# Two top-2 expert stages cut into blocks of 128 rows instead of 256

## The chip, the cores and the metric

The kernel runs on 1 core of a Trainium2 chip as one program. The metric is the device time of one execution in microseconds (us). Three executions of the kernel before took 8042.65, 8048.82 and 8052.29 us. Of its engines, TensorE is called PE (PEld is its weight load), VectorE DVE, ScalarE ACT, GpSimd POOL, and SyncE SP, the engine that issues most of the loads.

## The reference

The input is a graph of 3125 nodes with 256 features (all float32) and 50000 edges. The network has four layers; each is a graph part and a feed-forward part, both added to x. Three of the feed-forward parts matter here, because all three run through the same function of the kernel.

- Layer 1 (`_L1_ffn_ref`): a router picks the top 2 of 8 private experts for each row, and a shared expert is added. Each private expert is `gelu(x @ W1 + b1) @ W2 + b2` with W1 of 256 x 1024 and W2 of 1024 x 256.
- Layer 2 (`_L2_ffn_ref`): the top 2 of 6 experts, each of three 256 x 256 products: `h1 = relu(x @ w1 + b1)`, `h2 = relu(h1 @ w2 + b2)`, `out = h2 @ w3 + b3`.
- Layer 3 (`_L3_ffn_ref`): one hidden product that all experts share, `H = gelu(x @ W1 + b1)` with W1 of 256 x 1024, and then, for the one best of 8 experts, `H @ Wd[e] + bd[e]`.

In layers 1 and 2 there are 2 x 3125 = 6250 pairs of a row and an expert.

## The kernel before, in words

The kernel is a sequence of phases with a barrier between them. A feed-forward part is four phases: `logits`, `route`, `expert_blocks`, `combine`. The stages of layers 1, 2 and 3 have the names e3, e5 and e7 in what follows (the names that `program` gives them at lines 2440, 2451 and 2459).

`route` sorts the pairs by expert and pads each expert's rows to whole blocks. It writes the rows to a buffer in memory (xbuf), and the list of which expert owns which block to `k.block_expert` (lines 971 to 981). `block_count` (line 715) gives the number of blocks for the worst case, `(pairs + experts * (size - 1)) // size`, made even; that many blocks are always worked through. With 256 rows this is 32 for e3 and 30 for e5. Stage e7, with one pair a row, has had blocks of 128 rows (32 of them) already.

`expert_blocks` (line 1052) works through the blocks with two slots of buffers, so blocks 0, 2, 4, ... use slot 0 and blocks 1, 3, 5, ... slot 1. `NR` is the number of 128-row pieces in a block: 2 for 256 rows, 1 for 128. For each block:

- SP (lines 1089 to 1100) reads the expert's number and waits until the block that used the slot before is done, by the count `ydone`. Then it issues the load of the block's rows (L1094), the loads of the expert's weights and biases (L1097, L1098, L1099), and the last bias, spread over 128 partitions (L1100). The weights are loaded for every block, also where the expert is the same as before. Where the first product's weights are common to all experts (e7), they are loaded once (L1087).
- PE waits for all loads of the slot (L1118). It makes the hidden products (L1129), then turns the next block's rows (L1112, which needs only their load), and then makes the last product (L1139), 128 rows at a time.
- ACT applies the activation to each hidden piece of 128 columns (L1166) and copies the turned rows (L1157).
- DVE adds the last bias to each 128-row result (L1187) and raises `ydone`; POOL issues the store of the block (L1196).

The wait that governs the loads is this one:

```
sp.wait_ge(ydone, NR * B + 2 - NR)
sp.dma_start(xb[:, s, :, :], xbuf[ds(B * size, size), :]...
```

`ydone` starts at 2 and rises by `NR` with each block, so for both sizes the loads of block B are issued when block B-2 is done, that is when block B-1 can start.

Of the kernel before, what the change touches and what calls it, by code (L numbers as in the profile page):

```python
# [5 lines left out]
ALU = mybir.AluOpType  # L6
ACT = mybir.ActivationFunctionType
F32 = mybir.dt.float32
BF16 = mybir.dt.bfloat16
I32 = mybir.dt.int32  # L10
# [4 lines left out]
P = 128  # L15
N_NODES = 3125
# [15 lines left out]
CAP = 489  # L32
CAP_ROWS = 512
MAX_BLOCKS = 48
HEADS, STATES, TAPS, RANK = 4, 16, 4, 16
CH = 400
NCH = NP // CH
# [669 lines left out]
BLOCK = 2 * P  # L707
# [7 lines left out]
def block_count(pairs, experts, size=BLOCK):  # L715

    n = (pairs + experts * (size - 1)) // size
    return n + n % 2
# [183 lines left out]
def route(nc, name, k, lg, E, kind, xbuf, nblocks, beside=None, steps=0, share=None, size=BLOCK):  # L902
# [6 lines left out]
    with Phase(nc, name) as ph:  # L909
# [6 lines left out]
        nb_i, nb, endb, startb = ph.sb("nb_i", [P, EE], I32), ph.sb("nb", [P, EE]), ph.sb("endb", [P, EE]), ph.sb("startb", [P, EE])  # L916
        pos, base, kept, tgt = ph.sb("pos", [P, N]), ph.sb("base", [P, N]), ph.sb("kept", [P, N]), ph.sb("tgt", [P, N])
        tgt_u = ph.sb("tgt_u", [P, N], U32)
        trash = ph.sb("trash", [P, N])
        ow = ph.sb("ow", [1, MAX_BLOCKS])  # L920
        if share is not None:
            sh = SharedExpert(ph, k, share)
        pp = ph.ps("pp", [P, 2 * C, 512])
# [3 lines left out]
        with nc.Block() as b:  # L927
            @b.vector
            def _(v):
                c = Chain(v, dve)  # L930
# [34 lines left out]
                if kind == "capacity":  # L965
                    c(v.tensor_scalar(startb[:, :], k.expert[:, 0, 0:EE], float(CAP_ROWS), None, ALU.mult))
                    c(v.memset(ow[:, :], 0.0))
                    for e in range(EE):
                        c(v.memset(ow[:, e * (CAP_ROWS // BLOCK):(e + 1) * (CAP_ROWS // BLOCK)], float(e)))
                else:  # L970
                    c(v.tensor_scalar(nb[:, :], incl[:, N - 1, :], float(size - 1), None, ALU.add))
                    c(v.tensor_copy(nb_i[:, :], nb[:, :]))
                    c(v.tensor_scalar(nb_i[:, :], nb_i[:, :], size.bit_length() - 1, None, ALU.arith_shift_right))
                    c(v.tensor_copy(nb[:, :], nb_i[:, :]))
                    c(v.tensor_tensor_scan(endb[:, :], k.ones[:, 0:EE], nb[:, :], 0.0, ALU.mult, ALU.add))
                    c(v.tensor_tensor(startb[:, :], endb[:, :], nb[:, :], ALU.subtract))
                    c(v.memset(ow[:, :], -1.0))
                    for e in range(EE):
                        c(v.scalar_tensor_tensor(ow[:, :], k.iota[0:1, 0:MAX_BLOCKS], startb[0:1, e:e + 1], ow[:, :], ALU.is_ge, ALU.add))
                    c(v.tensor_scalar(startb[:, :], startb[:, :], float(size), None, ALU.mult))  # L980
                c(v.tensor_copy(k.block_expert[:, :], ow[:, 0:MAX_BLOCKS]))
                c(v.tensor_tensor(before[:, :, :], before[:, :, :], incl[:, :, :], ALU.add))
                c(v.tensor_tensor(before[:, :, :], before[:, :, :], tot[:, :, :], ALU.subtract))
                c(v.tensor_tensor(before[:, :, :], before[:, :, :], oh[:, :, :], ALU.mult))
# [218 lines left out]
def combine(nc, name, k, ybuf, C):  # L1203


    with Phase(nc, name) as ph:
        staged, landed, added, passed = ph.sem("staged"), ph.row_dmas(G, 16 * C * NG), ph.sem("added"), ph.sem("passed")
        ix, rows = ph.sb("ix", [P, G], U32), ph.sb("rows", [P, G, D])
        with nc.Block() as b:  # L1209
            @b.gpsimd  # L1210
            def _(g):
                with g.Fori(0, C * NG) as i:  # L1212
                    for j in range(G):
                        g.wait_ge(staged, i * G + j + 1)  # L1214
                        g.sem_inc(passed, 1)  # L1215
                        g.indirect_dma_start(rows[:, j, :], None, ybuf, bass.IndirectOffsetOnAxis(ap=ix[:, j:j + 1], axis=0)).then_inc(landed[j].sem, 16)  # L1216

            @b.vector
            def _(v):
                for j in range(G):  # L1220
                    v.tensor_copy(ix[:, j:j + 1], k.back[:, j:j + 1]).then_inc(staged, 1)  # L1221
                for q in range(C):
                    with v.Fori(0, NG) as i:
                        for j in range(G):
                            xt = k.x[:, ds(i * G + j, 1), :].rearrange("p a d -> p (a d)")
                            n = q * NT + i * G + j
                            landed[j].wait(v, 16 * i + 16 * q * NG + 16)
                            v.wait_ge(added, n)
                            v.scalar_tensor_tensor(xt, rows[:, j, :], k.coef[:, ds(i * G + j + q * NT, 1)], xt, ALU.mult, ALU.add).then_inc(added, 1)  # L1229
                            v.wait_ge(added, n + 1)  # L1230
                            v.tensor_copy(ix[:, j:j + 1], k.back[:, ds(i * G + j + q * NT + G, 1)]).then_inc(staged, 1)  # L1231
# [1145 lines left out]
def program(nc, a, out):  # L2377
    k = Keep()
    with ExitStack() as ctx:
        def sb(name, shape, dt=F32):  # L2380
            return ctx.enter_context(nc.sbuf_tensor(name, shape, dt))

        def dram(name, shape, dt=F32):
            return nc.dram_tensor(name, shape, dt).ap()
# [10 lines left out]
        by_dst = (sb("d_gi", [P, SP_], U32), sb("d_kl", [P, SP_]), None, sb("d_own", [1, SP_], I32))  # L2395
        k.lg, k.expert, k.small = sb("lg", [P, NT, 8]), sb("expert", [P, NT, 9]), sb("small", [P, NT])
        k.coef, k.back = sb("coef", [P, 3 * NT]), sb("back", [P, 3 * NT + G], U32)
        k.block_expert = sb("block_expert", [1, MAX_BLOCKS], I32)
        xbuf, ybuf = dram("xbuf", (MAX_BLOCKS * BLOCK + 3 * NP, D)), dram("ybuf", (MAX_BLOCKS * BLOCK, D))
        RowDma.values.clear()  # L2400
        nc.row_dma = [ctx.enter_context(nc.semaphore(f"row_dma{j}", n)) for j, n in enumerate(ROW_DMAS)]
# [7 lines left out]
        def edges(v):  # L2409
            return v.rearrange("(p c) -> p c", c=EC)  # L2410
# [5 lines left out]
        with ExitStack() as once:  # L2416
            sort_s = SlotScatter(nc, "by_src", once, rec_s, by_src, k.deg_out)
            sort_edges(nc, k, edges(a["src"]), edges(a["dst"]), edges(a["edge_weight"]), sort_s, sort_d, xbuf[0:MAX_BLOCKS * BLOCK, :], a["node_vec"], vrow)

# [13 lines left out]
        for l in range(3):  # L2433
# [1 line left out]
            transform(nc, f"t2{l}", k, k.t, a["L1_gnn_W"][l], "next" if l < 2 else "last", a["L1_gnn_b"][l], table)  # L2435
        normalise(nc, "n3", k, keep=True, dest=k.t)
        logits(nc, "g3", k, D, a["L1_ffn_Wr"], None, 8, k.lg[:, :, 0:8])
        nb = block_count(2 * N_NODES, 8)
        route(nc, "r3", k, k.lg[:, :, 0:8], 8, "shared", xbuf, nb, share=[a["L1_ffn_" + n][8] for n in ("W1", "b1", "W2", "b2")])
        expert_blocks(nc, "e3", k, xbuf, ybuf, nb, [(a["L1_ffn_W1"], a["L1_ffn_b1"], ACT.Gelu)], (a["L1_ffn_W2"], a["L1_ffn_b2"]))  # L2440
        combine(nc, "c3", k, ybuf[0:nb * BLOCK, :], 2)

        normalise(nc, "n4", k, scale=k.dinv, table=table, dest=k.t)
        aggregate(nc, "a4", k, by_dst, table, k.t, False)
# [1 line left out]
        batch_norm(nc, k, a["L2_gnn_gamma"], a["L2_gnn_beta"])  # L2446
        normalise(nc, "n5", k, keep=True, dest=k.t)
        logits(nc, "g5", k, P, a["L2_ffn_router_w2"], a["L2_ffn_router_b2"], 6, k.lg[:, :, 0:6], ACT.Relu, a["L2_ffn_router_w1"], a["L2_ffn_router_b1"])
        nb = block_count(2 * N_NODES, 6)
        route(nc, "r5", k, k.lg[:, :, 0:6], 6, "soft2", xbuf, nb)  # L2450
        expert_blocks(nc, "e5", k, xbuf, ybuf, nb, [(a["L2_ffn_expert_w1"], a["L2_ffn_expert_b1"], ACT.Relu), (a["L2_ffn_expert_w2"], a["L2_ffn_expert_b2"], ACT.Relu)],
                      (a["L2_ffn_expert_w3"], a["L2_ffn_expert_b3"]))
        combine(nc, "c5", k, ybuf[0:nb * BLOCK, :], 2)
        attention_layer(nc, k, a, by_dst, (xs, ys, zs, bc, heads, kl_rows, x_kept, y_kept))
        normalise(nc, "n7", k, keep=True, dest=k.t)
        logits(nc, "g7", k, 1024, a["L3_ffn_Wg"], a["L3_ffn_bg"], 8, k.lg[:, :, 0:8], ACT.Gelu, a["L3_ffn_W1"], a["L3_ffn_b1"])
        nb = block_count(N_NODES, 8, P)
# [64 lines left out]
```

## Time and profile before

| | us |
|---|---|
| median of the runs (lowest, highest) | 8048.82 (8042.65, 8052.29) |
| profiled execution | 8045.51 |
| its span in the profile | 8043.8 |
| PE busy in the span | 5186.8 (64%) |
| DVE busy | 3702.6 (46%) |
| POOL busy | 3884.8 (48%) |
| ACT busy | 1376.3 (17%) |

The phases follow each other, so these shares are averages over stages with different limits; a stage has to be read by itself. The times below are from the start of the span. A "granted clock" of 1.00 is TensorE at 2.4 GHz and 0.50 is 1.2 GHz. In the trace each float32 matmul stands as two MATMUL instructions.

### The profile page before, as it was taken

How to read it: one execution, taken by the hardware profiler on the slowest of the kernel's cores; microseconds unless marked ns; L12 is line 12 of the kernel's file. 1: busy time of each engine (PE TensorE's matmuls, PEld its weight loads, DVE VectorE, ACT ScalarE, POOL GpSimd, SP SyncE). 2: the span in 40 equal slices, each digit the busy share in tenths (PEclk: the TensorE clock that was granted, in tenths of full speed). 3: DMA queues.
4: the chain of work that ended last, by engine and by line, in shares of the span. 5: the costliest groups of instructions: out<-in, count | busy, mean ns of one | idle time of the engine just before them, and what ended most of it. 6: DMA issues, size and time to landing. Idle time of an engine off the chain costs nothing. (4 is left out here: it accounts for less than half of the span.)

```text
span 8043.8 us, 98143 instructions
## 1 busy us (share of the span) xinstructions
PE 5186.8 (64%) x20419; PEld 3885.2 (48%) x20420; DVE 3702.6 (46%) x10494; ACT 1376.3 (17%) x3853; POOL 3884.8 (48%) x3967
## 2 busy tenths in 40 slices
PE   1230688373388888889799778837465666617667
PEld 0120566262266666667588656625332444414356
DVE  8994455200355455454400155440445888853311
ACT  0000000110000000000223200012144555511233
POOL 3777777677577577577200267611432444410011
PEclk9999756686555665655899855568676777758788
DMA  2011333242233333334135433305432444420035
GB/s 91 2 10 18 89 105 84 69 124 48 74 104 105 95 105 105 95 104 102 46 121 192 151 102 104 91 26 181 143 98 62 125 126 124 112 84 11 7 121 163
DMA packets 434465, 747.31 MB, mean 93 GB/s; under 512 B 107906, under 2 KB 293772, under 8 KB 432204
## 3 DMA queue, kind: packets, MB, share of 16 engines
q0 software_dynamic: 169984, 401.24, 18.8%
q1 hardware_dynamic: 264396, 345.13, 13.3%
q8 instruction: 29, 0.48, 0.0%
q14 instruction: 56, 0.46, 0.0%
HBM read 645.17 MB, written 100.02 MB: 93 GB/s over the span
## 5 line engine op out<-in xcount | busy, mean ns | idle before, releaser
L594 PE MATMUL a_pa<-a_oh,a_rows 128*128 128x128 f32 x8320 | 2281.1, 429 | 663.2 <-DVE a_oh L558 288.8
L548 POOL DMA_INDIRECT a_rows<-table,a_ix x2080 | 1976.1, 950 | 830.7 <-issue 569.3
L594 PEld LDWEIGHTS a_pa<-a_oh,a_rows 128*128 128x128 f32 x8320 | 1797.6, 303 | 1146.8 <-issue 663.0
L581 DVE TENSOR_TENSOR t_sb<-t_sb,a_pa 128x256 f32 x2080 | 874.7, 421 | 1091.4 <-PE a_pa L594 995.7
L1808 POOL DMA_INDIRECT mx_at_rows<-heads,mx_at_ix x416 | 497.4, 1196 | 700.1 <-PE mx_at_pa L1854 587.9
L1187 DVE TENSOR_TENSOR e_ys<-e_py,e_bl 128x256 f32<-128x256 f32 x188 | 78.7, 424 | 1399.2 <-PE e_py L1139 1101.1
L1196 POOL DMA_DIRECT2D ybuf<-e_ys x110 | 74.3, 675 | 1013.7 <-DVE e_ys L1187 1008.1
L1129 PE MATMUL e_phid<-e_xt,e_w 128*128 128x256 f32 (+1 forms) x2800 | 531.7, 348 | 49.1 <-DMA e_bl<-in_L_ffn_expert_b 27.3
L196 POOL DMA_INDIRECT rec_s<-by_src_rstage,by_src_tstage x400 | 485.7, 1214 | 152.4 <-issue 107.7
L196 POOL DMA_INDIRECT rec_d<-by_dst_rstage,by_dst_tstage x400 | 474.5, 1186 | 153.6 <-issue 115.1
L1139 PE MATMUL e_py<-e_wl,e_h 128*128 128x256 f32 x2288 | 529.2, 388 | 6.9 <-DVE e_ys L1187 6.8
L644 ACT COPY t_ast<-t_sb 128x256 f32 x125 | 45.5, 403 | 2768.4 <-PEq L85 2727.6
L1129 PEld LDWEIGHTS e_phid<-e_xt,e_w 128*128 128x128 f32 x2800 | 461.5, 194 | 113.4 <-issue 63.4
L1139 PEld LDWEIGHTS e_py<-e_wl,e_h 128*128 128x128 f32 x2288 | 437.6, 196 | 67.5 <-DVE e_ys L1187 7.2
L1166 ACT ACTIVATE e_h<-e_phid,e_b 128x256 f32<-128x256 f32 (+1 forms) x760 | 329.2, 437 | 716.5 <-PE e_phid L1129 701.8
L502 PE MATMUL n_pt<-ident,n_stage 128*128 128x128 f32 x350 | 111.1, 446 | 517.2 <-DVE n_stage L478 516.7
L556 DVE TENSOR_SCALAR a_oh<-iota,d_kl 128x128 f32<-128x128 f32 x1696 | 362.0, 301 | 179.2 <-issue 179.2
L1854 PE MATMUL mx_at_pa<-mx_at_rows,mx_at_oh 128*128 128x260 f32 x832 | 297.2, 483 | 171.2 <-DVE y_sb L1790 87.1
L1875 ACT ACTIVATE mx_at_rows<-mx_at_rows 128x64 f32<-128x64 f32 x1664 | 406.3, 333 | 0.0
L397 PE MATMUL es_pdeg<-es_ohhi,es_ohlo 125*128 125x25 bf16 x800 | 145.8, 203 | 354.1 <-DVE es_ohhi L356 309.8
L502 PEld LDWEIGHTS n_pt<-ident,n_stage 128*128 128x128 f32 x350 | 51.7, 205 | 576.5 <-DVE n_stage L478 576.4
L2130 PE MATMUL mx_pmm<-mx_work,ident 128*128 128x320 f32 x640 | 301.1, 638 | 0.0
(472 smaller groups left out, 5951.4 us busy)
## 6 DMA issues: line engine op xcount, KB each, us to landing
mx_work<-bc SPq DMA_DIRECT2D x160, 320.0 KB, 3.4
e_w<-in_L_ffn_W SPq DMA_DIRECT2D x33, 1024.0 KB
a_rows<-table,a_ix POOLq DMA_INDIRECT x2080, 2.7
e_wl<-in_L_ffn_W SPq DMA_DIRECT2D x32, 1024.0 KB
e_wl<-in_L_ffn_Wd SPq DMA_DIRECT2D x32, 1024.0 KB
e_xb<-xbuf SPq DMA_DIRECT2D x78, 256.0 KB, 2.7
ybuf<-e_ys POOLq DMA_DIRECT2D x78, 256.0 KB, 4.0
e_w<-in_L_ffn_w SPq DMA_DIRECT2D x16, 1024.0 KB
```

The source lines that it names most:

```text
L196: g.indirect_dma_start(self.rec, bass.IndirectOffsetOnAxis(ap=self.tstage[:, j:j + 1], axis=0), self.rstage[:, j, :], None).then_inc(self. ...
L548: g.indirect_dma_start(rows[:, j, :], None, table, bass.IndirectOffsetOnAxis(ap=ix[:, j:j + 1], axis=0)).then_inc(landed[j].sem, 16)
L556: ins = v.tensor_scalar(oh[:, j, :], k.iota[:, 0:P], kl[:, ds(col, 1)], None, ALU.is_equal)
L581: v.tensor_tensor(acc[:, :, ts(tile, P)], acc[:, :, ts(tile, P)], pa[:, j % NB, 0:D].rearrange("p (k n) -> p k n", k=KD), ALU.add).then_in ...
L594: mm = pe.matmul(pa[:, j % NB, q * P:(q + 1) * P], rows[:, j, q * P:(q + 1) * P], oh[:, j, :], start=True, stop=True)
L1129: mm = pe.matmul(phid[:, (offs[l] + f) % NB, 0:size], ws[l][:, sl, q, f * P:(f + 1) * P], src, start=q == 0, stop=q == kt - 1)
L1139: mm = pe.matmul(py[:, (s * NR + n) % 2, 0:D], hs[-1][:, q, n * P:(n + 1) * P], wls[:, s, q, :], start=q == 0, stop=q == KL - 1)
L1166: a.activation(hs[l][:, f, :], phid[:, (offs[l] + f) % NB, 0:size], hidden[l][2], bias=bs[l][:, sl, f:f + 1]).then_inc(hact, 1)
L1808: g.indirect_dma_start(self.rows[:, h * STEP + j, :], None, self.table, bass.IndirectOffsetOnAxis(ap=self.ix[:, h, j:j + 1], axis=0)).then ...
L1854: pe.matmul(self.pa[:, j % 2, 0:ROW], self.oh[:, h * STEP + j, :], self.rows[:, h * STEP + j, :], start=True, stop=True).then_inc(self.sum ...
L1875: ins = a.activation(part, part, ACT.Identity, scale=self.rows[:, j, D + q:D + q + 1])
L2130: mm = pe.matmul(pmm[:, 2 * o + q, 0:H2], k.ident[:, :], dbx[:, s, o, q * H2:(q + 1) * H2], start=False, stop=False)
```

## The change

Stages e3 and e5 get `size=P` (128) in `block_count`, `route`, `expert_blocks` and `combine`. Their numbers of blocks become `block_count(6250, 8, 128)` = 56 and `block_count(6250, 6, 128)` = 54. The list of block owners grows from 48 to 64 entries. Nothing else is touched.

```diff
+BLOCK_SLOTS = 64
...
-        ow = ph.sb("ow", [1, MAX_BLOCKS])
+        ow = ph.sb("ow", [1, BLOCK_SLOTS])
...
-                        c(v.scalar_tensor_tensor(ow[:, :], k.iota[0:1, 0:MAX_BLOCKS], startb[0:1, e:e + 1], ow[:, :], ALU.is_ge, ALU.add))
+                        c(v.scalar_tensor_tensor(ow[:, :], k.iota[0:1, 0:BLOCK_SLOTS], startb[0:1, e:e + 1], ow[:, :], ALU.is_ge, ALU.add))
...
-                c(v.tensor_copy(k.block_expert[:, :], ow[:, 0:MAX_BLOCKS]))
+                c(v.tensor_copy(k.block_expert[:, :], ow[:, 0:BLOCK_SLOTS]))
...
-        k.block_expert = sb("block_expert", [1, MAX_BLOCKS], I32)
+        k.block_expert = sb("block_expert", [1, BLOCK_SLOTS], I32)
...
-        nb = block_count(2 * N_NODES, 8)
-        route(nc, "r3", k, k.lg[:, :, 0:8], 8, "shared", xbuf, nb, share=[...])
-        expert_blocks(nc, "e3", k, xbuf, ybuf, nb, [(a["L1_ffn_W1"], a["L1_ffn_b1"], ACT.Gelu)], (a["L1_ffn_W2"], a["L1_ffn_b2"]))
-        combine(nc, "c3", k, ybuf[0:nb * BLOCK, :], 2)
+        nb = block_count(2 * N_NODES, 8, P)
+        route(nc, "r3", k, k.lg[:, :, 0:8], 8, "shared", xbuf, nb, size=P, share=[...])
+        expert_blocks(nc, "e3", k, xbuf, ybuf, nb, [(a["L1_ffn_W1"], a["L1_ffn_b1"], ACT.Gelu)], (a["L1_ffn_W2"], a["L1_ffn_b2"]), size=P)
+        combine(nc, "c3", k, ybuf[0:nb * P, :], 2)
...
-        nb = block_count(2 * N_NODES, 6)
-        route(nc, "r5", k, k.lg[:, :, 0:6], 6, "soft2", xbuf, nb)
+        nb = block_count(2 * N_NODES, 6, P)
+        route(nc, "r5", k, k.lg[:, :, 0:6], 6, "soft2", xbuf, nb, size=P)
...
-                      (a["L2_ffn_expert_w3"], a["L2_ffn_expert_b3"]))
-        combine(nc, "c5", k, ybuf[0:nb * BLOCK, :], 2)
+                      (a["L2_ffn_expert_w3"], a["L2_ffn_expert_b3"]), size=P)
+        combine(nc, "c5", k, ybuf[0:nb * P, :], 2)
```

## Rows read from the trace of the kernel before

**Rows 1.** Windows of e3, e5, e7: busy us (count) by engine, PEclk, DMA share, GB/s.
```profile
4108.70:4567.40 458.70, 458.19 (x2172) 402.80 (x2172) 27.19 (x64) 138.16 (x287) 22.21 (x31) 0.99 0.55 185
5461.40:5675.80 214.40, 186.44 (x836) 144.43 (x836) 25.45 (x60) 72.69 (x149) 20.78 (x29) 0.98 0.63 194
7742.40:7986.80 244.40, 239.87 (x1598) 219.37 (x1598) 13.59 (x32) 117.92 (x302) 16.84 (x31) 0.99 0.56 181
```

**Rows 2.** Waits of SP's queue in e3: total us, times, longest.
```profile
SPq L1094 <- DVE e_ys L1187: 285.4, 30, 16.3
```

**Rows 3.** DMA issues of e3: count, KB each, median us to landing.
```profile
e_w<-in_L_ffn_W SPq DMA_DIRECT2D x32, 1024.0 KB
...
e_xb<-xbuf SPq DMA_DIRECT2D x32, 256.0 KB, 2.7
```

**Rows 4.** Timeline of e3: start us, us, engine, line, what, count, idle before.
```profile
4108.71 9.46 PE L1129 MATMUL e_phid<-e_xt,e_w 128*128 128x256 f32 x32 [6.92 <-DMA e_bl<-in_L_ffn_b]
...
4139.60 7.07 PE L1129 MATMUL e_phid<-e_xt,e_w 128*128 128x256 f32 x32
...
4140.41 0.38 SPq L1094 DMA_DIRECT2D e_xb<-xbuf  x1
```

**Rows 5.** Windows of 1 us in e3, PE alone: busy, PEclk, DMA share, GB/s.
```profile
4144.40:4145.40 1.00, 1.00 (x6) 1.00 1.00 393
...
4149.40:4150.40 1.00, 1.00 (x6) 1.00 0.15 44
```

**Rows 6.** Timeline of e7, PE and SP.
```profile
7742.40 6.76 PE L1129 MATMUL e_phid<-e_xt,e_w 128*128 128x128 f32 x32 [4.08 <-DMA e_bl<-in_L_ffn_bd]
...
7752.68 3.73 PE L1129 MATMUL e_phid<-e_xt,e_w 128*128 128x128 f32 x32
...
7851.27 3.83 PE L1129 MATMUL e_phid<-e_xt,e_w 128*128 128x128 f32 x32 [0.17 <-DMA e_bl<-in_L_ffn_bd]
...
7855.16 3.62 PE L1139 MATMUL e_py<-e_wl,e_h 128*128 128x256 f32 x16
7858.62 3.73 PE L1129 MATMUL e_phid<-e_xt,e_w 128*128 128x128 f32 x32
...
7866.31 3.83 PE L1129 MATMUL e_phid<-e_xt,e_w 128*128 128x128 f32 x32 [0.28 <-DMA e_bl<-in_L_ffn_bd]
```

**Rows 7.** Window of 1 us in e7, PE alone: busy, PEclk, DMA share, GB/s.
```profile
7865.40:7866.40 1.00, 0.72 (x4) 1.00 0.04 13
```

**Rows 8.** DMA issues of e7: the block's rows, KB and us to landing.
```profile
e_xb<-xbuf SPq DMA_DIRECT2D x13, 128.0 KB, 2.0
```

**Rows 9.** Timeline of e5, PE and SP.
```profile
5500.94 0.39 SPq L1094 DMA_DIRECT2D e_xb<-xbuf  x1
...
5504.07 0.50 SPq L1100 DMA_DIRECT2D e_bl<-in_L_ffn_expert_b  x1
...
5507.77 1.99 PE L1129 MATMUL e_phid<-e_xt,e_w 128*128 128x256 f32 x8 [1.42 <-DMA e_bl<-in_L_ffn_expert_b]
...
5513.89 1.89 PE L1129 MATMUL e_phid<-e_xt,e_w 128*128 128x256 f32 x8
...
5521.67 1.99 PE L1129 MATMUL e_phid<-e_xt,e_w 128*128 128x256 f32 x8 [1.60 <-DMA e_bl<-in_L_ffn_expert_b]
```

**Rows 10.** Timeline of e5, PE: blocks that start after idle time.
```profile
5478.57 3.67 PE L1129 MATMUL e_phid<-e_xt,e_w 128*128 128x256 f32 x8 [3.09 <-DMA e_bl<-in_L_ffn_expert_b]
...
5563.93 3.67 PE L1129 MATMUL e_phid<-e_xt,e_w 128*128 128x256 f32 x8 [2.03 <-DMA e_bl<-in_L_ffn_expert_b]
...
5593.50 1.99 PE L1129 MATMUL e_phid<-e_xt,e_w 128*128 128x256 f32 x8 [1.70 <-DMA e_bl<-in_L_ffn_expert_b]
```

**Rows 11.** A window of 1 us in e5, PE alone: busy, PEclk, DMA share, GB/s.
```profile
5479.00:5480.00 1.00, 1.00 (x4) 0.50 0.94 302
```

**Rows 12.** ACT's activations in e7: count, busy us, mean ns, idle before.
```profile
L1166 ACT ACTIVATE e_h<-e_phid,e_b 128x128 f32<-128x128 f32 x256 | 90.7, 367 | 79.5 <-PE e_phid L1129 64.8
```

**Rows 13.** Line 979, the list of owners: min, median, max ns.
```profile
L979 DVE SCALAR_TENSOR_TENSOR r_ow<-iota,r_startb,r_ow x22: 254/256/256, 3943.9 to 7688.4; 1x48 f32<-1x48 f32 x22
```

More of the change, by code:

```diff
@@ L2437, in program @@
         logits(nc, "g3", k, D, a["L1_ffn_Wr"], None, 8, k.lg[:, :, 0:8])
-        nb = block_count(2 * N_NODES, 8)
-        route(nc, "r3", k, k.lg[:, :, 0:8], 8, "shared", xbuf, nb, share=[a["L1_ffn_" + n][8] for n in ("W1", "b1", "W2", "b2")])
-        expert_blocks(nc, "e3", k, xbuf, ybuf, nb, [(a["L1_ffn_W1"], a["L1_ffn_b1"], ACT.Gelu)], (a["L1_ffn_W2"], a["L1_ffn_b2"]))
-        combine(nc, "c3", k, ybuf[0:nb * BLOCK, :], 2)
+        nb = block_count(2 * N_NODES, 8, P)
+        route(nc, "r3", k, k.lg[:, :, 0:8], 8, "shared", xbuf, nb, size=P, share=[a["L1_ffn_" + n][8] for n in ("W1", "b1", "W2", "b2")])
+        expert_blocks(nc, "e3", k, xbuf, ybuf, nb, [(a["L1_ffn_W1"], a["L1_ffn_b1"], ACT.Gelu)], (a["L1_ffn_W2"], a["L1_ffn_b2"]), size=P)
+        combine(nc, "c3", k, ybuf[0:nb * P, :], 2)
         normalise(nc, "n4", k, scale=k.dinv, table=table, dest=k.t)
```

## The prediction

> **What bounds the kernel now.** The phases run one after another, so only e3 and e5 and what they write for their neighbours can change. I read first the windows of the two stages and of e7, which already works in blocks of 128 rows, then the wait list of SP's queue, then the timeline of a few blocks, and last windows of 1 us for the DMA engines and the clock.
>
> The windows [rows 1] show three sorts of stage. In e3 PE is busy 458.2 of 458.7 us at a clock of 0.99: the stage is PE's, 458.7 / 32 = 14.3 us a block, and its DMA share of 0.55 leaves room. In e5 PE is busy 186.4 of 214.4 us, so something else takes part of it. In e7 PE is busy 239.9 of 244.4 us, 7.6 us a block. The loads explain the difference. SP's queue waited 285.4 us in e3 at L1094 for DVE's last add [rows 2]: loads are not issued far ahead but when block B-2 is done. So each slot runs a cycle of its own, load and then compute, and the two slots alternate on PE. I call L the time from the end of a block to the start of the next block of its slot when that start waits for its loads, and C the time in which PE works a block. If L is under C, PE sets C per block. If it is over, two blocks take L + C, and PE idles L - C once in each pair.
>
> The trace has this pattern twice. In e7 [rows 6] a block starts at 7851.27, the next at 7858.62 without idle time, and the third at 7866.31 after a wait for the last bias: C = 7.35, L = 7866.31 - 7858.62 = 7.69, a pair 15.04. The first block took 10.28 (7742.40 to 7752.68), being on the low clock; 10.28 + 7.35 + 15 x 15.04 = 243.2, against 244.4 measured. In e5 [rows 9] the starts are 5507.77, 5513.89 and 5521.67: C = 6.12, L = 7.78, pair 13.90. Both have the same load: 1024 KB of weights and 128 + 128 KB of rows and spread bias in e7, 768 + 256 + 128 in e5, and a store of 128 and 256 KB; 1408 KB each. So L goes with the bytes, and not with the number of DMAs (3 and 7).
>
> **Stage e3: what 128 rows remove.** PE's part falls from 14.3 to e7's C: the block has the same matmuls as one of e7, 16 hidden ones and 8 of the last product. I take C = 7.35 [rows 6]. 56 blocks of this would be 412 us, 47 less than now: fewer padding rows (7168 instead of 8192). What is late next is the load.
>
> **Stage e3: what they add.** The weights of a block stay 2048 KB [rows 3], and only its rows and its store fall from 256 to 128 KB each. L comes from two sides. (a) From e3 itself: a block ends at 4139.60, SP issues at 4140.41 (0.81) [rows 4], the DMA engines are still at 0.15 in the window from 4149.40, so they end near 4149.55 (9.15 after the issue) [rows 5]. From the last bytes to the first matmul e7 shows 7865.44 to 7866.31, 0.87 [rows 6, 7]. Together 10.83; less 262 thousand bytes at about 375 GB/s (the windows at full share show up to 393 [rows 5]), 0.7, it is 10.1. (b) From e7: 7.69, plus 1024 KB more at 375 GB/s, 2.8, is 10.5. I take 10.3. A pair takes 17.65, and PE idles 2.95 in it. The data of one load fills some 7.5 us of each 8.8, so the two slots' loads hardly meet.
>
> **The clock.** In e5 the blocks after 3.09 and 2.03 us of idle PE ran their first eight instructions in 3.67 us, the one after 1.70 us in 1.99 [rows 10], and the window in the first of them has a clock of 0.50 [rows 11]: 1.68 lost each time. An idle time of 2.95 once in each pair, where e3 now has none, is close to the worse of these. I take a loss in two pairs of three, 1.1 us a pair; none and every pair are the ends.
> The Trainium skill (TensorE: Matmul & The Clock Gate, "HAM oscillation") describes a thin-M matmul whose compute is shorter than its DMA wait and which starts every tile on the slow clock. By that every pair would pay 1.68, 16 us more in e3 than I take; this trace shows it for two of the waits in e5 and not for most.
>
> Sum for e3: 10.28 + 7.35 + 27 x (17.65 + 1.1) = 523.9, against 458.7: **+65**. Ends: L 10.1 without a loss 488.8 (+30); L 10.5 with one in every pair 545 (+86).
>
> **Stage e5.** C: at 128 columns a hidden instruction takes 0.112 (3.57 us for 32 before the turning starts) and one of the last product 0.216 ((7858.62 - 7855.16) / 16) [rows 6]. 16 hidden, 2 turning, 4 last: 1.8 + 0.2 + 0.9 = 2.9 us. The layers depend on each other through ACT, whose activation takes 0.37 [rows 12] and some 0.4 of signals around it; PE gets through only part of its work meanwhile, and stands about 0.75 in the two places. C = 3.65. L: 7.78 less 256 KB at 375 GB/s = 7.1. Its floor is the issue of the seven DMAs: 0.81, then 3.13 from L1094 to L1100 [rows 9], then 2.0 for 128 KB to land [rows 8]: 5.9. I take 6.9, nearest to e5's own rows. The pair is 10.55, PE idle up to 3.25 in it, less where the next block's rows land only after the hidden products: they are issued 0.81 after the block before ended and land 2.0 later, at 2.8, while the hidden products end near 2.4; that stall lies inside the idle time and costs nothing. Clock: half of a loss per pair, 0.9. The first two blocks take 10.6 (5.9 on the low clock, 3.65, 1.05 of that stall). 10.6 + 26 x 11.45 = 308, against 214.4: **+94**. Ends: L 5.9 and no loss 257 (+43); L 7.0 and every block late and slow, pair 12.95, 347 (+133).
>
> **The rest.** The list of owners has 16 more elements in some 16 DVE operations of 256 ns for 48 [rows 13]; even in proportion that is 1.4 us, and I take 0.3. The scatter into xbuf and the gather from ybuf move the same rows. ACT (138 us in e3) and DVE get shorter instructions, 56 and 54 times instead of twice 32 and 30; both idle mostly and stay hidden. POOL issues 48 stores more, each of some 0.5 us, all beside PE and DMA time.
>
> Sum: +65 + 94 = +159 on the profiled execution's 8045.5, so 8204.5; the median of the runs shown is 3.3 above that execution, so I predict **8208**.
>
> **Rivals.**
> (1) The loads are cheaper than my L. For this speaks 393 GB/s at full share [rows 5]; against it, that each load begins and ends with a part below it, which L of e7 contains. At the peak rate throughout, e3's 2.49 MB take 6.35, with 0.81, 1.0 to the first byte and 0.87 L = 9.0 and the pair 16.4: 460 us, no change; e5 at its floor +43. Result 8092.
> [...]
> (2) The clock never falls, since most waits in e5 did not bring it down: +35 and +71, result 8155. Against it: both idle times over 2 us did.
> (3) More than I count: two loads meet in the queue and every pair is slow, +86 and +133 and some more, 8275.
> (4) The other side, faster: loads are hidden and PE sets both stages. Then e3 is 56 x 7.35 + 3 = 415 (-44) and e5 54 x 3.65 + 3 = 200 (-14), result 7991. It decides from the point where L is under C. For e3 that needs 2.49 MB in some 5 us, 500 GB/s, which no window shows; e7 does not reach it even with half the bytes.
> (5) Gains and losses cancel, 8049: it needs (1) in e3 and more still in e5.
>
> **Numbers.** Forecast 0.60, (1) 0.08, (2) 0.17, (3) 0.10, (4) 0.03, (5) 0.02. 0.2%, 16 us, is about what a measurement can tell from no change. Slower by more 0.95, within 0.02, faster 0.03. The ends of the terms give 8122 and 8268; the range is 8120 to 8280, which leaves out most of (1), (4), (5) and the top of (3).
>
> **What would show it.** Right: in the profile after, each second block of e3 starts with PE waiting some 3 us for the last bias, starts of the same slot lie 17.6 to 19.3 us apart, DMA share in the stage near 0.85, mean clock under 0.95, weight bytes up by 24 x 2 MB and 24 x 0.75 MB; in e5 pairs of 10.5 to 12.5 us. Wrong: a PE that stays busy over 95% in e3, pairs under 16.5, or a stage e5 shorter than 250 us.

## The result and the profile after

The changed kernel takes 8293.84 us (8289.42 to 8299.74, four runs) against 8045.73 us (8039.77 to 8052.29, four runs) beside it: 1.0307 times as long, with an interval of 1.0295 to 1.0319. It is slower, as forecast, but by 248 us where 159 were forecast, and 14 us above the range's upper end.

The profiled execution took 8292.65 us. The windows below hold e3, e5 and e7 of the kernel after, with the columns of [rows 1].

```profile
4113.98:4669.74 555.76, 454.00 (x2798) 420.18 (x2798) 23.77 (x56) 179.20 (x503) 29.83 (x55) 0.92 0.74 246
5564.28:5927.32 363.04, 251.74 (x1186) 211.22 (x1186) 22.93 (x54) 98.98 (x269) 28.76 (x53) 0.76 0.59 172
7985.45:8233.99 248.54, 239.26 (x1598) 219.75 (x1598) 13.59 (x32) 118.21 (x302) 16.86 (x31) 0.99 0.56 179
```

e3 is 97.1 us longer than in [rows 1] and e5 148.6, together 245.7 of the 247.1 between the two profiled executions. (e7 is 4.1 longer, and the rest of the program 2.7 shorter.) PE is busy 454.0 of 555.8 us in e3: its work has hardly fallen, from 458.2, and 102 us of idle time have come in. In e5 the busy time has risen by 65 us for fewer rows. Its clock is 0.76, and that is most of it: the same 54 blocks at a clock of 0.99 (three_slots, below) keep PE busy for 200.5 us, 51 less.

What was moved is what the prediction counted. SP's queue waits for DVE as in [rows 2], now 54 times, and each load of [rows 3] but the rows' keeps its size:

```profile
SPq L1095 <- DVE e_ys L1188: 309.3, 54, 9.5
```
```profile
e_w<-in_L_ffn_W SPq DMA_DIRECT2D x56, 1024.0 KB
...
e_xb<-xbuf SPq DMA_DIRECT2D x56, 128.0 KB, 2.2
```

The timeline of e3 after, PE's hidden products and SP's first issues, with the columns of [rows 4, 6]:

```profile
4134.65 5.33 PE L1130 MATMUL e_phid<-e_xt,e_w 128*128 128x128 f32 x32 [4.33 <-DMA e_bl<-in_L_ffn_b]
4143.49 3.73 PE L1130 MATMUL e_phid<-e_xt,e_w 128*128 128x128 f32 x32
4154.48 5.46 PE L1130 MATMUL e_phid<-e_xt,e_w 128*128 128x128 f32 x32 [3.58 <-DMA e_bl<-in_L_ffn_b]
...
4384.62 3.73 PE L1130 MATMUL e_phid<-e_xt,e_w 128*128 128x128 f32 x32
4385.43 0.34 SPq L1095 DMA_DIRECT2D e_xb<-xbuf  x1
...
4395.47 3.83 PE L1130 MATMUL e_phid<-e_xt,e_w 128*128 128x128 f32 x32 [3.44 <-DMA e_bl<-in_L_ffn_b]
...
4654.75 3.84 PE L1130 MATMUL e_phid<-e_xt,e_w 128*128 128x128 f32 x32 [3.11 <-DMA e_bl<-in_L_ffn_b]
```

The blocks of slot 1 (4143.49, 4384.62) start without idle time; those of slot 0 start after some 3 to 4 us of waiting for the last bias (2.83 to 4.33, mean 3.73). From 4134.65 to 4654.75 there are 26 pairs of 20.00. L is 4154.48 - 4143.49 = 10.99 in the first pair shown and 10.85 in the one at 4384.62; over all pairs it is 11.15. The block after the wait runs its first 32 instructions mostly in 5.33 or 5.46 us (two take over 6) instead of 3.83, which is half the clock for a part of them: so 24 of the stage's 28 even blocks. The other four take 3.83 or 3.84, two of them shown; they followed 3.11 to 3.44 us of idle time, while a block after 2.83 was slow, so the length of the idle time alone does not decide it.

The timeline of e5 after, which answers to [rows 9, 10]:

```profile
5577.32 1.26 PE L1130 MATMUL e_phid<-e_xt,e_w 128*128 128x128 f32 x8 [3.68 <-DMA e_bl<-in_L_ffn_expert_b]
...
5699.88 2.07 PE L1130 MATMUL e_phid<-e_xt,e_w 128*128 128x128 f32 x8 [4.30 <-DMA e_bl<-in_L_ffn_expert_b]
...
5705.27 1.05 PE L1130 MATMUL e_phid<-e_xt,e_w 128*128 128x128 f32 x8
5706.08 0.34 SPq L1095 DMA_DIRECT2D e_xb<-xbuf  x1
...
5708.14 0.44 PE L1113 MATMUL e_pt<-ident,e_xb 128*128 128x128 f32 x2 [0.42 <-DMA e_xb<-xbuf]
...
5713.00 2.07 PE L1130 MATMUL e_phid<-e_xt,e_w 128*128 128x128 f32 x8 [3.55 <-DMA e_bl<-in_L_ffn_expert_b]
```

Here a pair takes 13.6 (from 5577.32 to 5917.31 are 25): L is 5713.00 - 5705.27 = 7.73, 7.97 over all, and the even block 5.39 instead of the 3.65 that was forecast, 5.63 over all. All 27 even blocks of the stage are slow, the one at 5577.32 only behind its first eight instructions. The eight first instructions of this one take 2.07 where those of the odd block take 1.05; a window of 0.5 us in them, PE alone, has the clock of 0.50 that [rows 11] has:

```profile
5700.00:5700.50 0.50, 0.50 (x3) 0.50 0.88 232
```

### The profile page after: what moved, and what is told of

It is laid out like the page before. It is cut to its first block and busy times, and to the rows that moved or that the text cites. A ratio compares the mean times of both kernels' runs of the same rounds, so it can differ in the third digit from the quotient of the medians.

```text
span 8290.9 us, 102977 instructions
## 1 busy us (share of the span) xinstructions
PE 5230.5 (63%) x21391; PEld 3955.4 (48%) x21392; DVE 3696.8 (45%) x10480; ACT 1443.6 (17%) x4189; POOL 3905.4 (47%) x4015
## 5 line engine op out<-in xcount | busy, mean ns | idle before, releaser
L1130 PE MATMUL e_phid<-e_xt,e_w 128*128 128x128 f32 (+1 forms) x3760 | 576.7, 317 | 231.0 <-DMA e_bl<-in_L_ffn_b 115.7
L1130 PEld LDWEIGHTS e_phid<-e_xt,e_w 128*128 128x128 f32 x3760 | 542.0, 216 | 280.1 <-issue 252.8
L1167 ACT ACTIVATE e_h<-e_phid,e_b 128x128 f32<-128x128 f32 (+1 forms) x1048 | 395.8, 381 | 890.3 <-PE e_phid L1130 849.0
L1140 PEld LDWEIGHTS e_py<-e_wl,e_h 128*128 128x128 f32 x2136 | 418.1, 202 | 62.4 <-DVE e_ys L1188 6.6
```

The costliest lines, as they stand in the source:

```text
L1130: mm = pe.matmul(phid[:, (offs[l] + f) % NB, 0:size], ws[l][:, sl, q, f * P:(f + 1) * P], src, start=q == 0, stop=q == kt - 1)
L1140: mm = pe.matmul(py[:, (s * NR + n) % 2, 0:D], hs[-1][:, q, n * P:(n + 1) * P], wls[:, s, q, :], start=q == 0, stop=q == KL - 1)
L1167: a.activation(hs[l][:, f, :], phid[:, (offs[l] + f) % NB, 0:size], hidden[l][2], bias=bs[l][:, sl, f:f + 1]).then_inc(hact, 1)
```

## The experiments

Below, e3 and e5 are the times from the first hidden product to the last add, from the profile of that kernel. Before: 458.6 and 214.4; after: 555.8 and 363.0. Four kernels (e3_only, warm, three_slots, three_slots_mixed) ran on another chip, where the kernel before itself takes 9030.22 us (it takes 8042.20 and 8045.78 on the two chips of the other runs): there the sums of neighbours in the graph parts take longer. The expert stages of the same form agree between the chips to within 1.5% (e3 550.8 and 555.8, e5 212.2 and 214.4), so stages are compared across chips, and totals only with the kernel before on the same chip.

### Each stage alone

e3_only takes the 128 rows back in e5, e5_only in e3.

```diff
-        nb = block_count(2 * N_NODES, 6, P)
+        nb = block_count(2 * N_NODES, 6)
...
-        combine(nc, "c5", k, ybuf[0:nb * P, :], 2)
+        combine(nc, "c5", k, ybuf[0:nb * BLOCK, :], 2)
```

> Only e3 is in blocks of 128 rows; e5 is as before, in 30 blocks of 256. Theory: the loss is made of two independent parts inside the two stages, each a pair time times its number of pairs. From the two traces e3 went from 458.7 to 555.5 us (+97) and e5 from 214.4 to 364.7 (+150). So this kernel should take the time of before plus 97: about 8145, with e5 at 214 and e3 at 555. Rival: part of the loss lies elsewhere (route, combine, a stage after), or e5 is slow because of what e3 leaves behind; then this kernel is off 8145 by more than 10 us, or its e5 is not at 214.

> Only e5 is in 54 blocks of 128 rows; e3 is as before, in 32 of 256. Theory: the loss of e5 is its own, +149 (214.4 to 363), and e3 stays at 458.6: 8043 + 149 = 8192, ratio 1.0185. With the +97 of e3 in 128 rows this is the whole loss. Rival: part of it comes only when both are changed.

e3_only: e3 is 550.8, e5 212.2. Its total is 9094.69 (two runs) against 9030.22, 1.0074 [1.0050, 1.0099], so +64 where +97 was expected, and 28 less than its stage lost (92); the two runs don't tell where. e5_only: e3 458.1, e5 363.5, total 8194.37 against 8045.78, 1.019 [1.0173, 1.0207], +148.6. In the profiles each stage loses by itself what it loses in the changed kernel, within 5 us. The total bears this out for e5; for e3 alone the missing 28 us stay open.

### The clock: matmuls into the idle time

Before PE waits for the loads of a block of slot 0, it multiplies the identity by itself 14 times, into a part of PSUM that nothing reads. The wait for the turned rows (`xt_copied`), which came after that for the loads, now comes first.

```diff
+                    pe.wait_ge(xt_copied[s], i + 1)
+                    for _ in range(fill if s == 0 else 0):
+                        pe.matmul(pt[:, 0, KD * size:KD * size + P], k.ident[:, :], k.ident[:, :], start=True, stop=True)
                     pe.wait_ge(loaded[s], 16 * n_ld * i + 16 * n_ld)
-                    pe.wait_ge(xt_copied[s], i + 1)
```

> The changed kernel, and before each even block of e3 and e5 PE multiplies the identity by itself 14 times (28 instructions of 0.112 us, 3.1 us) into unused columns, ahead of its wait for the loads; the waits of the even blocks are some 3.8 us. Nothing else is changed. Theory: the second part of the loss is the clock. In e3 24 of 28 even blocks took 8.9 us instead of 7.35, and in e5 nearly all 5.6 instead of some 3.7. With PE busy in the wait the clock stays at 1.00: C of the even blocks falls to 7.35 and 3.7, e3 by 27 x 1.47 = 40 and e5 by 26 x 1.9 = 49, in all about -89, 8205 us. Rival 1: the clock does not fall because of the wait, C stays, the time stays at 8294 or rises by what filler sticks out. Rival 2: a shorter C only brings the two slots' loads closer together and L grows by as much as C falls; gain under 40.

> The changed kernel with PE kept busy ahead of the even blocks' waits by 14 products of the identity; run once before on another chip, where the granted clock was 1.00 in both stages and they took 515.7 and 308.6 us instead of 555.8 and 363.0. Theory: the clock's part of the loss is 40 + 54 = 94 of 247. Then 8293 - 94 = 8199 here, ratio to before 1.019. Rival: the gain was that chip's; ratio near 1.03.

Windows of e3 and e5 of warm_again, columns as before:

```profile
4118.04:4636.84 518.80, 501.65 (x3554) 468.05 (x3554) 23.77 (x56) 179.21 (x503) 29.82 (x55) 0.99 0.81 263
5530.98:5835.88 304.90, 277.82 (x1916) 232.91 (x1914) 22.93 (x54) 93.67 (x269) 28.75 (x53) 1.00 0.70 204
```

The granted clock is back at 0.99 and 1.00 (from 0.92 and 0.76), and the stages fall by 37 and 58 us. (warm, on the other chip, has 515.7 and 308.6.) In the timeline of warm the filler stands where the idle time was, and the next block runs at full clock without a wait:

```profile
5116.91 3.29 PE L1121 MATMUL e_pt<-ident 128*128 128x128 f32 x28
5120.03 3.74 PE L1132 MATMUL e_phid<-e_xt,e_w 128*128 128x128 f32 x32
```

Totals: 8199.81 against 8045.78, 1.0192 [1.0175, 1.0209], and on the other chip 9170.55 against 9030.22, 1.0153 [1.0127, 1.0178]. So some 95 of the 246 us are the clock, and 150 are left with the clock at full speed. The loads are not shorter by it. From the start of an odd block to the next even one it is now 6.97 in e5, not 7.97, but the odd block starts 0.76 later than the end of the even block, since now it too waits for its loads, as the timeline of warm_again shows:

```profile
5603.55 1.15 PE L1132 MATMUL e_phid<-e_xt,e_w 128*128 128x128 f32 x8 [0.83 <-DMA e_bl<-in_L_ffn_expert_b]
...
5610.69 1.15 PE L1132 MATMUL e_phid<-e_xt,e_w 128*128 128x128 f32 x8 [0.30 <-DMA e_bl<-in_L_ffn_expert_b]
```

From the last matmul of an even block to the next even block it is 7.73 in e5 where the changed kernel has 7.82, and 11.09 in e3 where it has 11.03. Nearly all that was gained is the even blocks' full clock.

### Loads off the path: a third slot

The semaphores, rows, weights and biases get three slots, and the loads of block B go into slot B % 3, while the form of SP's wait stays as it was.

```diff
-        loaded, once, xloaded = ph.sems("loaded", 2, "hardware"), ph.sem("once", "hardware"), ph.sems("xloaded", 2, "hardware")
-        xb, xt = ph.sb("xb", [P, 2, NR, D]), ph.sb("xt", [P, 2, KD, size])
+        loaded, once, xloaded = ph.sems("loaded", NS, "hardware"), ph.sem("once", "hardware"), ph.sems("xloaded", NS, "hardware")
+        xb, xt = ph.sb("xb", [P, NS, NR, D]), ph.sb("xt", [P, 2, KD, size])
...
-                        pe.wait_ge(ydone, B * NR + n + 1)
+                        pe.wait_ge(ydone, B * NR + n + 1 + J)
```

`ydone` starts higher by one block (`J` is `NR`), and so the loads of block B are issued when block B-3 is done, one block sooner. three_slots has 128 rows in e3 and e5, three_slots_mixed 128 in e3 and 256 in e5, three_slots_256 256 in both, and three_slots_all is the mixed one with three slots in e7 as well.

> The changed kernel with three instead of two slots for the loaded rows, weights and biases of e3 and e5 (block B's loads are issued when block B-3 is done, one block time earlier); the loops are unrolled by six. Theory: the loss is the cycle of load and compute per slot. With three slots a load has two block times to land, so e3 is set by PE (7.35 a block) or by the DMA engines, which were busy 15.3 us for two loads, 7.65 each: 56 x 7.65 + 10 = 438, 117 less than changed. e5 is set by SP's issue of seven DMAs a block, 4.4 us: 54 x 4.4 + 8 = 246, 119 less. Total about 8058. Rival: the loads are limited by what the DMA engines move (2.49 MB a block at the stage's 300 GB/s is 8.3 us, and 5.3 in e5); then e3 is 475, e5 294, total 8143. If L were pure latency with nothing shared, e3 would be at 56 x 7.35 = 412 + 10 and the total near 8040.

> Three slots in e3 and e5, e3 in 56 blocks of 128 rows, e5 in 30 blocks of 256 as before. Theory: e3 438 us as in the kernel with three slots in both; e5 leaves the pair of 13.9 us and is set by PE, 6.05 a block, 30 x 6.05 + 8 = 190 instead of 214. Total 8048 - 21 - 24 = about 8003: faster than before and than changed. Rival (DMA engines limit): e3 475, e5 at 30 x 5.3 or PE's 190, total near 8040, no clear gain over before.

> The kernel before (both stages in blocks of 256 rows), with three slots for the loads of e3 and e5. Theory: with the loads out of the way each stage is set by PE. e3 was that already, so it stays at 458; e5 goes from 214 to 183 as in the mixed kernel. Total 31 below before, ratio 0.996 to 0.997. With the mixed kernel (e3 408) this gives what blocks of 128 rows are worth in e3 by themselves: 50 us, the padding rows left out. Rival: three slots help e3 at 256 rows too (then part of the mixed kernel's gain is not due to 128 rows).

> The mixed kernel (e3 in 128 rows, e5 in 256, three slots in both) with three slots in e7 as well. e7 took 244 to 248 us for 32 blocks with a pair of 15.04; PE needs 7.25 to 7.3 a block: 32 x 7.3 + 4 = 238, some 7 us less. Total 82 + 7 = 89 below before, ratio 0.989. Rival: e7's waits are too short to matter, no difference from the mixed kernel that can be measured in the total (the stage length in the trace tells).

Windows of three_slots (e3, e5):

```profile
4847.70:5255.63 407.93, 407.38 (x2798) 383.92 (x2798) 23.81 (x56) 178.85 (x503) 29.80 (x55) 1.00 0.99 335
6335.62:6574.20 238.58, 200.46 (x1186) 153.13 (x1186) 22.94 (x54) 93.38 (x269) 28.72 (x53) 0.99 0.85 262
```

and of three_slots_all (e3, e5, e7):

```profile
4113.00:4520.95 407.95, 407.39 (x2798) 383.91 (x2798) 23.79 (x56) 179.15 (x503) 29.80 (x55) 1.00 0.99 335
5416.96:5599.89 182.93, 178.91 (x836) 143.64 (x836) 25.47 (x60) 72.80 (x149) 21.10 (x29) 0.99 0.74 228
7657.84:7892.68 234.84, 234.28 (x1598) 220.71 (x1598) 13.59 (x32) 108.52 (x292) 16.83 (x31) 0.99 0.60 189
```

| | e3 | e5 | total | before beside it | ratio |
|---|---|---|---|---|---|
| three_slots | 407.9 | 238.6 | 9006.58 | 9030.22 | 0.9974 [0.9963, 0.9985] |
| three_slots_mixed | 408.1 | 183.0 | 8938.10 | 9030.22 | 0.9894 [0.9878, 0.9911] |
| three_slots_256 | 458.9 | 182.9 | 8024.29 | 8042.20 | 0.9979 [0.9969, 0.9988] |
| three_slots_all | 407.9 | 182.9 | 7958.73 | 8042.20 | 0.9898 [0.9882, 0.9915] |

With the same 56 blocks e3 falls from 555.8 to 407.9, where 438 was expected, with the DMA engines as the limit: PE is busy 407.38 of 407.93 us, and a block takes 7.28, close to the C of 7.35 from [rows 6], so PE is the limit. So 148 us of the changed e3 came from the wait for loads and the clock that it cost, and the smaller blocks by themselves are worth 408 against 459, 51 us. The third slot gives the old e3 nothing (458.9), since PE bound it; it has value there only together with the small blocks. The DMA share of 0.99 says that the DMA engines have little room left either.

e5 is another matter. With three slots it takes 238.6 in 54 blocks and 182.9 in 30 blocks, and 214.4 before. In three_slots SP's queue has no wait in e5 at all; its timeline has one block's seven DMAs and the next block's first one:

```profile
6453.68 0.34 SPq L1103 DMA_DIRECT2D e_xb<-xbuf  x1
...
6456.67 0.42 SPq L1109 DMA_DIRECT2D e_bl<-in_L_ffn_expert_b  x1
6457.99 0.34 SPq L1103 DMA_DIRECT2D e_xb<-xbuf  x1
```

The distance is 4.31, and 238.58 / 54 = 4.42: the stage is SP's issuing, DMA after DMA (3.0 of the 4.31 from the first to the last, 1.3 to the next block's first); 30 blocks instead of 54 nearly halve that. Three slots also take e7 from 244.4 to 234.8 us. three_slots_all is the best kernel of these, 83 us under the one before; its total and that of three_slots_mixed come from different chips and can't show the gain of e7.

The stage gains of three_slots_256 (31.5 in e5) are more than its total shows, 18 (interval 10 to 25); where the rest went stays open.

### What L is made of

L had missed in both stages. Four kernels, each with two slots and 128 rows, change one part of a load each.

In odd_keeps only slot 0 loads weights and biases anew, so two loads of weights can never meet; slot 1 still loads its rows and stores its results. The odd blocks compute with expert 0, so their own experts are left out.

```diff
+                        if keep and s:
+                            continue
```

> The changed kernel, but in e3 and e5 the odd slot loads its weights and biases once, ahead of the loop, and keeps them (so odd blocks compute with expert 0; that part of the computation is left out). The even slot loads as before: same bytes, same instructions. Measured for the changed kernel: L (end of an even block to the start of the next even one when it waits) 11.15 us in e3 and 7.96 in e5, where I forecast 10.3 and 6.9. Theory: the difference is the neighbour. The odd slot's load is issued 7.35 us (e3) or 4.4 us (e5) after the even slot's, while that is still moving, and its rows, store and first weights take their share of the DMA engines. With the odd slot's weights gone, L falls to 10.1 to 10.5 in e3 and to 6.9 to 7.2 in e5. Rival: L is the load's own (fixed parts and bytes), I only read too little from the trace of before; then L stays at 11.1 and 7.9.

Windows of e3 and e5:

```profile
4113.04:4663.18 550.14, 450.50 (x2798) 417.97 (x2798) 23.78 (x56) 178.89 (x503) 29.82 (x55) 0.93 0.42 136
5562.17:5925.20 363.03, 251.41 (x1186) 211.59 (x1186) 22.94 (x54) 98.89 (x269) 28.70 (x53) 0.76 0.36 104
```

The DMA share falls from 0.74 to 0.42 and from 0.59 to 0.36, and the stages stay where they were to within 6 us. L is 11.08 and 7.97: the other slot's weights are not what makes it long. Its rows and its store, 256 KB that are still moved near the end of slot 0's load, are not excluded by this kernel; the next one, which triples the rows of both slots, speaks against them, though there slot 1's rows are issued 0.7 us later than in the changed kernel.

rows_tripled loads 384 rows of xbuf with each block instead of 128, 256 KB more than after, and works on the first 128.

```diff
-                        sp.dma_start(xb[:, s, :, :], xbuf[ds(B * size, size), :].rearrange("(n p) d -> p n d", p=P)).then_inc(xloaded[s], 16)
+                        sp.dma_start(xb[:, s, :, :], xbuf[ds(B * size, 3 * size if wide else size), :].rearrange("(n p) d -> p n d", p=P)).then_inc(xloaded[s], 16)
```

> The changed kernel, and each block of e3 and e5 loads 384 rows instead of 128 (384 KB instead of 128; the surplus rows are not used). My forecast subtracted 256 KB (half of the rows and half of the store) from the load at 375 GB/s, 0.7 us of L in each stage; the odd slot's loads, as the neighbour, have been shown not to explain why this did not come. Theory now: rows and store move in the first 2 to 3 us of a load, in which the DMA engines are not full anyway (66 to 236 GB/s in the windows there, while SP issues the DMAs one after another and the small bias is moved), and so their bytes are nearly free. Then 256 KB more per load leave L at 11.1 to 11.3 in e3 (stage 550 to 560 us) and at 7.9 to 8.2 in e5 (363 to 370). Rival (every byte costs at 375 GB/s, and something else makes up for it): L 11.8 and 8.6, stages 573 and 381.

Windows of e3 and e5:

```profile
4107.31:4653.44 546.13, 454.01 (x2798) 413.97 (x2798) 23.76 (x56) 181.33 (x503) 29.80 (x55) 0.93 0.81 277
5547.88:5913.83 365.95, 257.28 (x1186) 214.97 (x1186) 22.91 (x54) 99.04 (x269) 28.72 (x53) 0.75 0.66 208
```

e3 is 546.1 (9.6 less than after), e5 365.9 (2.9 more); L is 10.85 and 7.84, both a little shorter. The rows themselves land later (3.5 us after their issue in e3, where after has 2.2), and PE waits for them inside the odd block, but the last bias lands no later. 262 thousand bytes more in each load cost nothing, which at 375 GB/s would have been 0.7 a pair, 19 us in e3. The reason can be seen in 1-us windows of the kernel after, PE alone, columns as in [rows 5], around the load that is issued from 4385.43 on:

```profile
4385.00:4386.00 1.00, 1.00 (x12) 1.00 0.00 0
4386.00:4387.00 1.00, 1.00 (x12) 1.00 0.46 138
4387.00:4388.00 1.00, 1.00 (x12) 1.00 1.02 140
4388.00:4389.00 1.00, 1.00 (x9) 1.00 0.72 274
4389.00:4390.00 1.00, 1.00 (x7) 1.00 1.09 438
4390.00:4391.00 1.00, 1.00 (x6) 1.00 0.97 358
```

The rows are the first DMA, and in the windows from 4386.00 to 4389.00 the load moves 138, 140 and 274 GB/s, against 358 to 438 later. More rows go into time in which the rate is low anyway. The same can be seen in the kernel before, which loads twice the rows. These are the third and the fourth microsecond after SP's issue, before and after:

```profile
4142.40:4143.40 1.00, 1.00 (x6) 1.00 1.04 272
4143.40:4144.40 1.00, 1.00 (x7) 1.00 1.01 369
...
4387.42:4388.42 1.00, 1.00 (x12) 1.00 0.82 115
4388.42:4389.42 1.00, 1.00 (x7) 1.00 1.02 414
```

In the third the kernel before moves more than twice as much; in the fourth both are at the high rate. Half the rows did not bring the weights any sooner.

In bias_once all biases are loaded before the loop, so a load has two DMAs less in e3 (3 instead of 5) and three less in e5 (4 instead of 7).

```diff
-    n_ld = 2 + 2 * len(per)
+    n_ld = 1 + len(per) if bias_once else 2 + 2 * len(per)
...
-                        sp.dma_start(bls[:, s, :], bl[ds(e, 1), :].rearrange("a n -> (a n)").partition_broadcast(P)).then_inc(loaded[s], 16)
+                        if not bias_once:
+                            sp.dma_start(bls[:, s, :], bl[ds(e, 1), :].rearrange("a n -> (a n)").partition_broadcast(P)).then_inc(loaded[s], 16)
```

> The changed kernel with all biases of e3 and e5 loaded once, ahead of the loop, for expert 0 (the experts' own biases are left out). A block's load then has the rows and the weights only: three DMAs instead of five in e3, four instead of seven in e5, and 128 KB less. By bytes alone (375 GB/s) L falls by 0.35 us in both stages: 10.8 and 7.6. Theory on e5: with 1152 KB in seven DMAs L is set by SP's issue of them (3.1 us from the first to the last) and the last one's landing, which is why 256 KB less brought nothing; then three fewer DMAs, some 1.4 us of issue, bring L to about 6.5. Rival: the neighbour's load explains e5 too, and L falls to 7.6 only. In e3, where the last issue comes long before the last byte, L falls to 10.8 in both; to 10.2 or less if the spread bias is slow for its size.

Windows of e3 and e5:

```profile
4111.60:4642.06 530.46, 447.69 (x2798) 412.93 (x2798) 23.78 (x56) 179.23 (x503) 29.80 (x55) 0.93 0.74 244
5539.73:5833.68 293.95, 224.43 (x1186) 179.02 (x1186) 22.94 (x54) 96.76 (x269) 28.72 (x53) 0.89 0.60 188
```

L falls by 0.7 to 10.41 in e3, and by 1.65 to 6.31 in e5; the stages by 25 and 69, the latter with a clock that rises from 0.76 to 0.89 as the idle time gets shorter.

In e5 the idle time before an even block is now 1.89 to 2.70, and 12 of the 27 even blocks run at full clock, in 3.64 to 3.71 us. One of them follows a longer idle time than one that is slow:

```profile
5596.88 1.15 PE L1137 MATMUL e_phid<-e_xt,e_w 128*128 128x128 f32 x8 [2.38 <-DMA e_wl<-in_L_ffn_expert_w]
...
5616.56 2.07 PE L1137 MATMUL e_phid<-e_xt,e_w 128*128 128x128 f32 x8 [1.89 <-DMA e_wl<-in_L_ffn_expert_w]
```

The two or three DMAs carry few of the bytes, by which L would have fallen by 0.35 (the estimate ahead of the run); they cost more than that, above all in e5. Whether it is their number or the form of the spread bias, one row written to 128 partitions, is not separated.

Then they might cost less ahead of the weights. bias_first issues rows, spread bias, small bias, weights, in all expert stages.

```diff
+                        sp.dma_start(bls[:, s, :], bl[ds(e, 1), :].rearrange("a n -> (a n)").partition_broadcast(P)).then_inc(loaded[s], 16)
+                        for q, (w, bias, _) in enumerate(hidden):
+                            if w.shape[0] > 1:
+                                sp.dma_start(bs[q][:, s, :], bias[ds(e, 1), :, :].rearrange("a p f -> p (a f)")).then_inc(loaded[s], 16)
                         for q, (w, bias, _) in enumerate(hidden):
                             if w.shape[0] > 1:
                                 sp.dma_start(ws[q][:, s, :, :], w[ds(e, 1), :, :].rearrange("a (k p) f -> p (a k) f", p=P)).then_inc(loaded[s], 16)
-                                sp.dma_start(bs[q][:, s, :], bias[ds(e, 1), :, :].rearrange("a p f -> p (a f)")).then_inc(loaded[s], 16)
                         sp.dma_start(wls[:, s, :, :], wl[ds(e, 1), :, :].rearrange("a (k p) n -> p (a k) n", p=P)).then_inc(loaded[s], 16)
-                        sp.dma_start(bls[:, s, :], bl[ds(e, 1), :].rearrange("a n -> (a n)").partition_broadcast(P)).then_inc(loaded[s], 16)
```

> The changed kernel with the DMAs of a block issued in another order, in all expert stages: rows, the spread last bias, the small biases, then the weights (before: the weights first and the spread bias last). Same DMAs, same bytes. With all biases loaded once L fell by 0.7 us in e3 and by 1.65 in e5, more than the 0.35 of their bytes. Theory: it is the small DMAs' place behind the weights, the last of them being issued late and moved slowly (windows of 211 GB/s and less at the end of a load); ahead of the weights they would ride in the slack at the start. Then L falls by 0.3 to 0.7 in e3 (stage 532 to 548) and 0.5 to 1.2 in e5 (330 to 350). Rival: what counts is how many DMAs SP has to issue before the last weight; then the weights come later by 0.5 us and L is the same or up by up to 0.5 (e3 550 to 565, e5 363 to 375).

e3 takes 591.1 (+35), e5 363.6 (+0.6), and e7 260.5 where after has 248.5. L is 12.00 in e3 (0.85 more) and 8.15 in e5 (0.18 more), and all 28 even blocks of e3 are slow, so that a pair there costs 1.3 more. The theory that the small DMAs cost by their place at the end is out; that they delay the weights, as the rival ahead of the run had it, fits.

The totals of these four kernels, one run each, follow the stages: 8289.24, 8289.29, 8209.16 and 8350.74 in the order told, where the kernel before takes 8042.20 (odd_keeps, bias_once) and 8045.78.

## Why the prediction was wrong

**Right.** What bounds the stages: two blocks take L + C, PE idles once in a pair, and what is added is all in e3 and e5. three_slots shows it from the other side, since with the loads off the path e3 takes 408 where the prediction's "56 blocks of this would be 412" stands. C = 7.35 at full clock holds (the odd block from 4384.62 lasts until 4395.47 - 3.44, which is 7.41). ACT's activation took 368 ns where [rows 12] has 367, and an operation on the list of owners 273 where [rows 13] has 256. The rest of the program was put at 0.3 us, and apart from the stages it differs by -2.7 plus e7's 4.1. Rival (4) fell: L is above C in e3 by nearly 4. So did rivals (1), (2) and (5). Of the signs, the wait for the last bias, the clock under 0.95 (0.92) and the added loads came; the pairs are longer than the signs had them (20.0 and 13.6), and the DMA share lower (0.74 where 0.85 was expected).

**Wrong: L, by one step in both stages.** For e3 side (a) gave 10.83 from e3's own rows, and then "less 262 thousand bytes at about 375 GB/s [...], 0.7". That subtraction is the step that failed. The rows ride in the first microseconds of a load, where the rate is not full, and rows_tripled shows that as many bytes of rows put back cost nothing either (half of the subtracted bytes were the store, which no run changed by itself). Measured is 11.15, 0.32 above the 10.83 without it; of the 0.85 by which the 10.3 missed, 0.53 is this step, and where the 0.32 comes from stays open. The same step stands in e5 as "7.78 less 256 KB at 375 GB/s = 7.1", from which 6.9 was taken, nearer to the floor; measured is 7.97, close to the 7.78 of [rows 9] (over all pairs of e5 before, L is 7.90). Side (b) added bytes to e7's L and failed because L does not go with the bytes alone: "So L goes with the bytes, and not with the number of DMAs (3 and 7)" rested on two stages whose L agreed, and bias_once, which takes away three small DMAs of seven, takes 1.65 off e5's L with few bytes. The missed L is 0.85 x 27 = 23 us in e3 and 1.07 x 26 = 28 in e5.

**Wrong: what the clock costs.** "I take a loss in two pairs of three" for e3 and "half of a loss per pair" for e5. The size of one loss, 1.68, was right for e3, where a slow even block takes 8.97 and one at full clock 7.34. But it comes in 24 of 28 pairs. In e5 it comes in all 27, and the mean even block is 5.63, where 3.65 and a loss of 0.9 had been allowed; at full clock such a block takes 3.70 (bias_once), so one loss is 1.9 there, also more than the 1.68 taken from blocks of 256 rows. Most of the miss in e5, 20 of 28 us, is the share. The missed amount is (8.82 - 8.45) x 27 = 10 us in e3 and (5.63 - 4.55) x 26 = 28 in e5. [Rows 10] pointed that way: the idle times of 3.09 and 2.03 cost the clock and that of 1.70 did not, and I expected 3 us of idle time and still took less than all. But no limit follows from them: in bias_once 12 idle times of up to 2.38 were free and one of 1.89 was not. The rule of the Trainium skill (TensorE: Matmul & The Clock Gate, "HAM oscillation"), which stood beside the forecast with 16 us more, is nearer to what the trace has than my share was. Its case is a matmul with less compute than wait, which e3 is not (some 16 us of work in a pair against 3.7 of idle time), and four blocks escaped here, so "every" is not borne out in full.

These four terms add up to 33 and 56 us; the stages missed by 555.8 - 523.9 = 32 and 363.0 - 308 = 55. They are linked: a longer L is a longer idle time, and with the shorter idle times of bias_once fewer blocks were slow. That is why rival (3), "more than I count", with 8275, came closest, and why its chance of 0.10 was too small. Its mechanism was only half right: nearly every pair is slow, but the other slot's weights don't make a load longer (odd_keeps).

## What to carry to other kernels

Where a slot's load is released by the end of its own last block, halving the block's work nearly doubles how often the same load is paid (32 times to 56 here); compute L + C for a pair before the change, and give the loads another slot first: then the small blocks that lost 97 us gained 51. Take L whole from the rows of a stage with the same load, and don't subtract bytes at the peak rate from it when they ride in its start. If PE is to idle 3 to 4 us in each turn, price the slow clock in all of them (here 51 of 55 even blocks; e3 of e3_only had 22 of 28); at 1.9 to 2.7 us it was 15 of 27. And where a block's load is many small DMAs, ask for the issuing queue's own time: it set e5 in 128 rows once no wait was left in it.

## What was not expected of the hardware

- 14 float32 matmuls on the identity in each pair's idle time brought the granted clock from 0.76 to 1.00 in e5 and took 58 us off a stage of 363, though PE had then more to do than before (278 against 252 us busy).
- The length of the idle time does not tell by itself whether the clock falls: idle times of 3.11 to 3.44 us left it up four times in e3 of the changed kernel, while one of 2.83 there and one of 1.89 in e5 of bias_once brought it down.
- A DMA share of 0.99 at 335 GB/s over 408 us (three_slots, e3) shows that the loads of this kernel can run beside one another at nearly the full rate; with two slots the same loads reached 246.
- Two chips ran the same program in 8046 and 9030 us, with the expert stages alike within 1.5%.
